# Last stage of a four-layer network on one Trainium2 core: a part's two halves made in quarters, a step's weights in two transfers

## What is computed

```python
cross = x[..., idx_a] * x[..., idx_b]            # 496 pairs of the 32 columns
feat = jnp.concatenate([x, x * x, cross], axis=-1)   # 560 features
return jnp.einsum('bcij,cijo->bcio', feat, weight)
x = x + _L3_conv_ref(_gn(x), L3_conv_weight, L3_conv_idx_a, L3_conv_idx_b)
```

## Time and profile before

| | |
|---|---|
| profiled execution | 732.94 us, its span 731.1 us |
| median of three runs | 734.14 us |
| last stage, first own term to the end | 497.3 to 731.1 us |
| busy over the whole span | PE 497.6, DVE 566.7, ACT 431.5, POOL 420.1 us |
| DMA traffic | 209.09 MB, mean 286 GB/s |
| a load of a step's weights, issue to landing | 9.0 us median |

### The profile page before, as it was taken

How to read it: one execution, slowest core, us unless ns; L and a number is a source line. 1 busy time by engine, 2 the same in 40 slices (tenths; PEclk the granted TensorE clock), 3 DMA queues, 4 the chain that set the end, 5 groups by cost and what they waited for, 6 DMA issues and landing times.

```text
span 731.1 us, 53320 instructions
## 1 busy us (share of the span) xinstructions
PE 497.6 (68%) x24392; PEld 388.3 (53%) x24392; DVE 566.7 (78%) x709; ACT 431.5 (59%) x717; POOL 420.1 (57%) x653
## 2 busy tenths in 40 slices
PE   3546656609479999806666623626898888887898
PEld 4535655509368888605656521204565555554565
DVE  4799999898833635389999989955688788887787
ACT  5359999574011212317999938324567766666665
POOL 3388885004445651029888200537779878878672
PEclk9858889758799999955888975966899999999999
DMA  8949999500179999946999930015789999999996
GB/s 329 422 146 397 400 399 397 231 0 1 32 275 376 379 390 392 412 192 230 395 395 398 368 138 0 1 26 163 270 302 402 368 353 406 364 340 384 333 387 246
DMA packets 38882, 209.09 MB, mean 286 GB/s; under 512 B 7216, under 2 KB 14384, under 8 KB 18352
## 3 DMA queue, kind: packets, MB, share of 16 engines
q1 hardware_dynamic: 29376, 201.67, 72.2%
q10 hardware_dynamic: 9216, 6.30, 2.8%
q0 software_dynamic: 240, 0.53, 0.2%
HBM read 193.79 MB, written 4.19 MB: 271 GB/s over the span
## 4 chain that ended last, share of the span: by engine, by line
PE 37%; DVE 19%; DMA 13%; issue 11%; ACT 9%; POOL 8%; ACTq 2%; SPq 0%; DVEq 0%; POOLq 0%
PE psum L902 15%; PE psum L1015 7%; DMA wring<-in_pairs 6%; PE psum L989 5%; PE psum L926 5%; ACT signs L510 4%; DMA beyond<-state_b 4%; POOL xn_ring L267 3%; ACT state_b L640 2%; DVE state_b L862 2%; DVE state_a L807 2%; PE psum L1001 2%; DMA beyond<-state_a 2%; POOL state_a L372 2%; ACTq L526 2%
## 5 line engine op out<-in xcount | busy, mean ns | idle before, releaser
L862 DVE TENSOR_TENSOR state_b<-psum,state_b 128x512 f32<-128x512 f32 x256 | 167.6, 686 | 52.2 <-ACT state_b L640 48.2
L902 PE MATMUL psum<-signs,near 64*32 64x96 f16 (+3 forms) x6528 | 128.8, 221 | 98.1 <-DMA beyond<-nothing 37.8
L640 ACT ACTIVATE state_b<-psum 128x512 f32<-128x512 f32 x256 | 142.0, 595 | 81.3 <-PE psum L989 77.0
L902 PEld LDWEIGHTS psum<-signs,near 64*32 64x32 f16 (+1 forms) x6528 | 116.1, 105 | 106.8 <-issue 106.3
L747 DVE TENSOR_REDUCE abs_sums<-wring 128x1 f32<-128x2048 f32 x64 | 142.8, 2276 | 0.1
L510 ACT ACTIVATE signs<-wring 128x2304 f16<-128x2304 f32 x64 | 134.9, 2108 | 0.0
L1015 PE MATMUL psum<-state_b,wring 128*32 128x32 f32 x8192 | 104.5, 201 | 11.0 <-issue 5.3
L1015 PEld LDWEIGHTS psum<-state_b,wring 128*32 128x32 f32 x8192 | 86.9, 112 | 40.6 <-issue 21.6
L902 PE MATMUL psum<-wring,near 64*32 64x96 f32 (+5 forms) x3264 | 96.2, 242 | 14.8 <-DMA beyond<-nothing 10.5
L989 PE MATMUL psum<-signs,sel 64*128 64x512 f16 x516 | 88.1, 395 | 26.2 <-POOL signs L428 13.9
L428 POOL COPY signs<-wring 64x512 f16<-64x512 f16 x130 | 85.7, 659 | 30.7 <-PE psum L989 24.3
(11 more groups left out here) (153 smaller groups left out, 881.6 us busy)
## 6 DMA issues: line engine op xcount, KB each, us to landing
wring<-in_w SPq DMA_DIRECT2D x96, 1152.0 KB, 10.2
wring<-in_pairs SPq DMA_DIRECT2D x64, 1152.0 KB, 9.0
state_a<-in_x SPq DMA_DIRECT2D x8, 512.0 KB, 9.9
beyond<-state_b ACTq DMA_DIRECT2D x112, 32.0 KB, 5.9
wring<-signs SPq DMA_DIRECT2D x56, 64.0 KB, 4.9
out<-state_a SPq DMA_DIRECT2D x7, 512.0 KB, 10.8
beyond<-state_a ACTq DMA_DIRECT2D x56, 32.0 KB, 6.1
beyond<-nothing ACTq DMA_DIRECT2D x24, 32.0 KB, 4.7
```

The lines of the kernel that those rows point to most:

```text
L640: act.activation(left[:, n % LSLOTS, :], psum[:, n % ASLOTS, :], ACT.Copy, scale=1.0 / HALF_SCALE / HALF_SCALE).then_inc(left_made, 1)
L862: dve.tensor_tensor(feats[:, n % FSLOTS, :], psum[:, ASLOTS + n % BSLOTS, :], left[:, n % LSLOTS, :], ALU.mult).then_inc(feats_made, 1)
L902: last = pe.matmul(psum[g * B:(g + 1) * B, bank, (a * C) % 512:(a * C) % 512 + (b - a) * C], acts[q, j, s, k, :], weights[q, j, kind, s, ( ...
```

## The change

`high` and `low` of parts 1 to 7 are each made in four operations over 256 columns. For an odd group the four of `high` stand ahead of tiles 7, 9, 11 and 14 of ScalarE's stream, and those of `low` ahead of tiles 8, 10, 12 and 15 of VectorE's. Part 1's, made before the loop until now, stand ahead of tiles 2, 3, 4, 6 and 3, 4, 6, 7 of group 0. Counts of `hi_split` and `lo_split` follow: part 0 gives one, each later part four (`split_of`).

A step's weights are laid out with own terms first, and come in two transfers: own weights and tiles 0 and 1 (1280 floats to a partition), then tiles 2 and 3 (1024 floats). The first half of step k + 4's goes out after two mixes of step k, the second after four. TensorE waits for the first before own terms and for the second before tile 2.

```diff
-STEP = WSTEP + OWN
+STEP = OWN + WSTEP
+HSTEP = OWN + WSTEP // 2
+QUARTERS = 4
+HIGH_AT = ((2, 3, 4, 6), (7, 9, 11, 14))
+LOW_AT = ((3, 4, 6, 7), (8, 10, 12, 15))
...
+        def split_of(i):
+            return 1 + QUARTERS * i
+
+        def next_part(n, places):
+
+            grp, t = n // GT, n % GT
+            i = grp // 2 + 2 if grp % 2 else 1
+            if (grp == 0 or grp % 2) and i < V and t in places[grp % 2]:
+                return i, places[grp % 2].index(t)
+            return None
...
-            def load_pairs(k):
-                sp.dma_start(wsteps[:, k % WSLOTS, :], w_pairs[k]).then_inc(pairs_in[k % WSLOTS], 16)
+            def load_pairs(k, half):
+                cols, landed = ((slice(0, HSTEP), pairs_in), (slice(HSTEP, STEP), pairs_rest))[half]
+                sp.dma_start(wsteps[:, k % WSLOTS, cols], w_pairs[k, :, cols]).then_inc(landed[k % WSLOTS], 16)
...
-                    sp.wait_ge(made[k], 1 if i == 0 else i + 1)
+                    sp.wait_ge(made[k], split_of(i))
...
-                sp.wait_ge(mixed, PT * (k + 1))
-                if k + WSLOTS < NK:
-                    load_pairs(k + WSLOTS)
+                for half in range(2):
+                    sp.wait_ge(mixed, PT * k + PT // 2 * (half + 1))
+                    if k + WSLOTS < NK:
+                        load_pairs(k + WSLOTS, half)
...
-            def high(i):
+            def high(i, quarter):
 
                 act.wait_ge(part_made, i + 1)
                 if i >= 2:
                     act.wait_ge(parts_in[i - 2], 16 * 2 * G)
-                act.activation(hi_lo[:, i % 2, 0, :], xn[:, i % 2, :], ACT.Copy, scale=HALF_SCALE).then_inc(hi_split, 1)
+                cols = slice(quarter * (PART // QUARTERS), (quarter + 1) * (PART // QUARTERS))
+                act.activation(hi_lo[:, i % 2, 0, cols], xn[:, i % 2, cols], ACT.Copy, scale=HALF_SCALE).then_inc(hi_split, 1)
...
-            high(1)
             for n in range(TILES):
                 grp, t = n // GT, n % GT
                 if t % (GT // 2) == PT + 1 and grp + 1 < NGROUP:
                     square_own(grp + 1, t // (GT // 2))
-                if t == GT // 2 + 5 and grp % 2 and grp // 2 + 2 < V:
-                    high(grp // 2 + 2)
+                if next_part(n, HIGH_AT):
+                    high(*next_part(n, HIGH_AT))
...
-                dve.wait_ge(hi_split, i + 1)
-                dve.scalar_tensor_tensor(hi_lo[:, i % 2, 1, :], xn[:, i % 2, :], HALF_SCALE, hi_lo[:, i % 2, 0, :],
+                dve.wait_ge(hi_split, split_of(i - 1) + quarter + 1)
+                cols = slice(quarter * (PART // QUARTERS), (quarter + 1) * (PART // QUARTERS))
+                dve.scalar_tensor_tensor(hi_lo[:, i % 2, 1, cols], xn[:, i % 2, cols], HALF_SCALE, hi_lo[:, i % 2, 0, cols],
                                          ALU.mult, ALU.subtract).then_inc(lo_split, 1)
...
-            low(1)
             for n in range(TILES):
                 grp, t = n // GT, n % GT
-                if t == GT // 2 + 7 and grp % 2 and grp // 2 + 2 < V:
-                    low(grp // 2 + 2)
+                if next_part(n, LOW_AT):
+                    low(*next_part(n, LOW_AT))
...
+                    if t % PT == PT // 2:
+                        pe.wait_ge(pairs_rest[t // PT], j * 16 + 16)
                     mix(j, t)
```

More of the change, by code:

```diff
@@ L198, in build @@
         pairs_in = sems("pairs_in", WSLOTS)
+        pairs_rest = sems("pairs_rest", WSLOTS)
         step_begun = sem("step_begun")
@@ L311, in _ @@
             for k in range(WSLOTS):
-                load_pairs(k)
+                for half in range(2):
+                    load_pairs(k, half)
             signed(2 * CHUNKS - 1)
@@ L462, in normalise_part @@
                     pool.wait_ge(squared, 4 * (i - 1))
-                    pool.wait_ge(hi_split, i - 1)
-                    pool.wait_ge(lo_split, i - 1)
+                    pool.wait_ge(hi_split, split_of(i - 2))
+                    pool.wait_ge(lo_split, split_of(i - 2))
                     pool.wait_ge(own_copied, 4 * OWN_OPS * (i - 1))
@@ L836, in low_half_of, with low @@
                                          ALU.mult, ALU.subtract).then_inc((lo_half, lo_split)[half], 1)
-            def low(i):
+            def low(i, quarter):
                 dve.wait_ge(part_made, i + 1)
-                dve.wait_ge(hi_split, i + 1)
-                dve.scalar_tensor_tensor(hi_lo[:, i % 2, 1, :], xn[:, i % 2, :], HALF_SCALE, hi_lo[:, i % 2, 0, :],
+                dve.wait_ge(hi_split, split_of(i - 1) + quarter + 1)
+                cols = slice(quarter * (PART // QUARTERS), (quarter + 1) * (PART // QUARTERS))
+                dve.scalar_tensor_tensor(hi_lo[:, i % 2, 1, cols], xn[:, i % 2, cols], HALF_SCALE, hi_lo[:, i % 2, 0, cols],
                                          ALU.mult, ALU.subtract).then_inc(lo_split, 1)
@@ L993, in own_terms @@
             def own_terms(s):
-                w = wsteps[:, s, WSTEP:STEP].rearrange("p (u c o) -> p u c o", u=2, c=C4)
+                w = wsteps[:, s, 0:OWN].rearrange("p (u c o) -> p u c o", u=2, c=C4)
                 for c in range(C4):
@@ L1009, in mix @@
                 pe.wait_ge(feats_made, j * GT + (t + 1))
-                wt = wsteps[:, s, 0:WSTEP].rearrange("p (t c g o) -> p t c g o", t=PT, c=C4, g=G)
+                wt = wsteps[:, s, OWN:STEP].rearrange("p (t c g o) -> p t c g o", t=PT, c=C4, g=G)
                 f = feats[:, t % FSLOTS, :].rearrange("p (g c b) -> p g c b", g=G, c=C4)
@@ L1084, in _rearranged @@
     own3 = own3.transpose(4, 0, 2, 5, 6, 3, 1, 7).reshape(NK, P, OWN)
-    pairs3 = np.concatenate([pairs3, own3], axis=2)
+    pairs3 = np.concatenate([own3, pairs3], axis=2)
     p = np.arange(P)
```

## The result

The changed kernel took 729.86 us (median of 13 runs) against 734.63 for the kernel before, a ratio of **0.9921** with a 95% interval of 0.9896 to 0.9946, so 0.8% shorter in this timing. The forecast was 731.5, in a range of 727.0 to 737.5. From its first own term to the end of the span that stage took 731.15 - 497.32 = 233.8 us before and 726.19 - 492.54 = **233.7 us** after. The 4.8 us between the two profiles lie ahead of the code that was changed.

What follows compares the result with a forecast made beforehand. After 574 us two bounds were taken to lie close together, work at 27.35 us a period and transfers at 28.1 to 28.9. Terms of +3.5 - 5.6 - 0.5 = -2.6 us from 734.14 gave 731.5 us, range 727.0 to 737.5.

Steps and rivals of the forecast that it cites:

- Bounds: Last stage after 574 us: work at 27.35 us a period and transfers at 28.1 to 28.9 lie close together.
- The first piece's wait: Odd groups: ScalarE stands ahead of tile 7 until GpSimd makes the part, 2.3 us five times, 1.0 in the first.
- The odd group, 15.4 us: Odd group of four steps with the wait: 12.72 + 2.7 = 15.4 us against 14.63; pieces add nothing on top.
- work +3.5 us: Sum over odd groups: +0.8 us for each of five parts and -0.5 for the first.
- Waits for weights: TensorE's stands for late weights in the last stage fall from 7.5 us to 1.9, so -5.6 us.
- the last period: End of the last stage, 25.97 us against 25.44 of work: another 0.5 us goes.
- Transfers, 28.1 to 28.9 us a period: Transfer time for an even and an odd group after 574 us, from DMA share and bytes; 29.2 were measured.
- rival D: Odd groups: the wait for the part isn't met, transfers alone decide at 28.1 us a period; -6.7, 727.4 us; chance 0.12.
- The sum: Whole change, all in the last stage: +3.5 - 5.6 - 0.5 = -2.6 us, so 731.5 us.
- A: The main forecast, waits for weights 0.8 to 3.0 us, odd group 15.0 to 15.8; 729 to 734 us; chance 0.42.
- Rival B: Last stage: transfers decide in both kernels, a period stays at 29.2 to 29.4 us; total 734.3 us; chance 0.20.
- What a measurement can tell: Whole kernel: a measurement tells about 0.2%, 1.5 us, so 732.7 to 735.6 us counts as the same.

Runs made afterwards that it cites:

- light loads: From step 4 on each load transfer brings 128 columns, the rest stale; groups 1 to 12: kernel before 163.5 us, changed 169.7, pieces later 159.8.
- pieces later: Changed kernel with odd groups' `high` at tiles 10, 11, 12, 14 and `low` at 11, 12, 14, 15; ratio to before 0.9971, stage 234.4 us.
- halves alone: Changed kernel's two weight transfers, with `high` and `low` whole at tiles 13 and 15, part 1's ahead of the loop; ratio to before 0.9990.

## Why the prediction was right, and where it wasn't

*Bounds.* Right: work and transfers lie close together. Work of 164.1 us in groups 1 to 12 was 163.5 with light loads; the 7.5 us that the transfers cost were 8.1.

*The first piece's wait.* Right, in place and size: 2.3 us, five times in the first profile, and in the next too (12.3 us in sum with the short sixth). The wait of 1.0 in the first odd group was absent in the first profile and the third, and 0.7 in the second. In the first the part was made at 517.01 and ScalarE ended tile 6 at 517.87, since TensorE was late there: the granted clock was 0.5 until 515.6, 1.7 us into that group.

*The odd group, 15.4 us.* Right for a TensorE at full clock (15.42, 15.43 and 15.41 with light loads), and for the claim that pieces of `low` fit in VectorE's idle time behind it. **The step that failed is its closing line**, work +3.5 us: the sum took TensorE's durations at full clock although it put a stand of over 2 us in its stream. At full clock the work grew by 3.9. Each fall to the lower level costs another 0.8 to 1.2 us of a group (16.21 to 16.63 against 15.42), there were four in the first profile, and the work grew by 7.5.

*Waits for weights.* -5.6 was forecast, from 7.5 to 1.9: in groups 1 to 12 they went from 8.1 to nothing. The mechanism was right: with longer groups the transfers keep up. But the two misses cancel, and the near hit of the total in the stage is luck: +7.5 - 8.1 = -0.6 us in groups 1 to 12, where +3.5 - 5.6 = -2.1 was forecast. The 0.5 us that were to go in the last period didn't: TensorE stood 1.5 us for weights ahead of step 54, and the rest of the stage behind step 52 took 40.7 to 41.3 us against 40.2 and 40.6.

*Transfers, 28.1 to 28.9 us a period.* Too small, and it is the second step to mend: over steps 20 to 51 no kernel with full transfers took less than 29.0 a period, and pieces later took 29.6, of which the last two 30.7 each. The estimate took the 29.2 us of the kernel before down by the DMA share, and for the lower bound by bytes as well; the share can't be read so closely, and the rate at a share of 1.00 depends on what is moved (297 and 424 GB/s above). How much of the 29.6 is shorter rows, and how much TensorE's stands, isn't shown. Had the wait for the part been absent (rival D), I would have forecast 727.4; that kernel's stage was 234.4, no better than the others.

*The sum.* -2.6 us; the stages' means say -0.4, within the own range of A only by its edge, and the measured -4.8 of the medians isn't explained by it. That the first timing, 729.86, lies 1.6 us from the forecast is luck: 4.8 of the 4.95 us between the two profiled executions lie ahead of the stage. Rival B, transfers decide in both kernels and nothing much moves, has the stage's size right, with 29.2 to 29.4 us a period. Its cause isn't what the profile after shows: in groups 1 to 12 TensorE waits for no weights, and 16.3 + 12.7 = 29.0 us of its own work fill the period. A DMA share of 0.99 stands there beside it, so the share doesn't tell which of the two binds.

*What a measurement can tell.* I took 0.2%; a kernel against itself gave 0.9971, and the changed program 0.9921 to 1.0008.

*Rule against two transfers.* 60 more transfers made no stage longer by a measurable amount: halves alone 234.7 against 234.5. The Trainium skill (DMA: Bandwidth & Descriptors, Anatomy of one DMA) states about 2.0 us fixed for one transfer, for GpSimd's way of issuing. On SyncE's queue, where a first half lands 9.4 us after its issue and several transfers are on their way at a time, nothing of the 120 us that 60 of them would be in series is seen.

## What to carry to other kernels

Where a piece of work is moved ahead in an in-order stream, look up when its input is made: with light loads four small pieces at the right place made 9.9 us less work than four at the wrong place (2.2 of it by two falls of the clock), with one whole operation in between. Where two bounds lie within 5% of each other, measure each by taking the other away (light transfers, narrow copies) before paying for a gain on one of them. Where the sum puts a stand into TensorE's stream, price the fall of its clock as well. And compare a kernel with itself, and stage by stage, before a ratio of 0.99 is believed.

## What was not expected

Behind a stand of TensorE of 2.1 us in an otherwise busy stage its clock often falls from 2.4 to 1.2 GHz, for 3.4 us each time. It happened at four, four and five of the five such stands (2.0 to 2.2 us) in the three profiles of the changed kernel, and with the same program and light loads at two of five. What decides which stands are followed by a fall isn't settled here. Behind stands of 1.4 and 1.6 us ahead of own terms in the second profile of the kernel before it fell too; in the first, behind one of 1.5, it didn't.

Transfers between partitions of SBUF, in rows of 2 KB, cost the transfers beside them more than their bytes: with a spread on its way the kernel before moved 297 GB/s at a DMA share of 1.00, where loads in rows of 9 KB alone moved 424 at 1.01. By an estimate from these rates that spread cost 1.8 us beyond the time of its bytes, which is 1.2. Whether the rows' length or the way between partitions makes the difference wasn't tried.
